# A post-LN transformer block: next batch's q and k made in units 5 and 6, a unit's first step reordered, and the last maxima and sums moved from the FFN's first tile into unit 7

## The reference

```python
def attention(x, w_qkv):                      # x: 8 x 1024 x 512
    q, k, v = split_heads(x @ w_qkv)          # 16 heads of 32
    probs = softmax(q @ k.T / sqrt(512))
    return join_heads(probs @ v)
def fp4_quant_dequant(x):                     # blocks of 16
    scale = maximum(max(abs(block)) / 6, 1e-12)
    return nearest_on_grid(abs(block) / scale) * sign(block) * scale
x = layernorm(x + attention(x, w_qkv))
h = silu(fp4_linear(x, w_gate)) * fp4_linear(x, w_up)     # 512 -> 1408
x = layernorm(x + fp4_linear(h, w_down))                  # 1408 -> 512
```

## Time and profile before

| | us |
|---|---|
| median of 3 runs (lowest, highest) | 4126.7 (4125.9, 4129.7) |
| the profiled execution's own time | 4124.7 |
| its span, first to last instruction | 4123.0 |
| TensorE busy (share of the span) | 3806.5 (92%) |
| VectorE busy | 3051.1 (74%) |
| GpSimd busy | 2283.0 (55%) |
| ScalarE busy | 1749.4 (42%) |
| mean granted clock of TensorE | 0.977 |

### The profile page before, as it was taken

The page is one execution under the profiler, slowest core; times in us unless marked ns, Lnnn a source line. Parts: engine busy times, 40 slices in busy tenths (PEclk is TensorE's granted clock), DMA queues, the critical chain, the costliest instruction groups (busy, mean ns, idle before and its releaser), DMA issues. The chain is left out here.

```text
span 4123.0 us, 61806 instructions
## 1 busy us (share of the span) xinstructions
PE 3806.5 (92%) x22985; PEld 1728.9 (42%) x22985; DVE 3051.1 (74%) x4929; ACT 1749.4 (42%) x3104; POOL 2283.0 (55%) x1446
## 2 busy tenths in 40 slices
PE   3489999999999999999999999999999999999999
PEld 2234344433543345433453434443454334534344
DVE  8866687676876778666786668776786667866787
ACT  3345522664235632455225552265423553245522
POOL 4468722885239832588227862298424883268722
PEclk9689999999999999999999999999999999999999
DMA  4110110111010110111101101101101111010110
GB/s 163 44 58 26 29 50 24 35 32 50 23 35 18 40 44 24 30 32 32 47 19 40 29 21 54 31 22 32 53 22 32 26 34 48 19 37 24 32 49 21
DMA packets 106560, 152.56 MB, mean 37 GB/s; under 512 B 28177, under 2 KB 55569, under 8 KB 106129
## 3 DMA queue, kind: packets, MB, share of 16 engines
q1 hardware_dynamic: 106256, 148.49, 11.6%
HBM read 76.28 MB, written 19.66 MB: 23 GB/s over the span
## 5 line engine op out<-in xcount | busy, mean ns | idle before, releaser
L571 DVE TENSOR_REDUCE mx<-R 128x1 f32<-128x512 f32 x2080 | 1334.4, 686 | 662.6 <-PE R L663 654.6
L1186 ACT ACTIVATE arena<-SC 128x512 f32<-128x512 f32 x1344 | 749.7, 603 | 413.9 <-PE SC L1438 411.0
L1512 PE MATMUL SC<-wgu,split 128*128 128x512 f16 (+1 forms) x3456 | 724.0, 364 | 0.6
L1084 POOL TENSOR_TENSOR wd<-wd,arena 128x1024 f32<-128x1024 f32 x208 | 485.7, 2357 | 31.0 <-ACT arena L1186 29.9
L1110 POOL TENSOR_TENSOR arena<-arena,sc_h 128x704 f32<-128x704 bf16 (+2 forms) x136 | 176.1, 1312 | 576.8 <-DVE arena L496 576.8
L1186 ACT ACTIVATE wd<-SC 128x512 f32<-128x512 f32 x704 | 399.8, 603 | 201.1 <-PE SC L1438 196.9
L1512 PEld LDWEIGHTS SC<-wgu,split 128*128 128x128 f16 x3456 | 338.3, 98 | 343.8 <-issue 12.6
L663 PE MATMUL R<-ks_even,qs_even 96*128 96x512 bf16 x1056 | 398.5, 399 | 88.6 <-issue 45.3
L1227 ACT ACTIVATE arena<-SC,gain 128x512 f32<-128x512 f32 (+1 forms) x192 | 125.1, 652 | 775.0 <-PE R L1512 390.7
L643 PE MATMUL R<-xT,wqkv 128*128 128x512 bf16 x1632 | 429.3, 386 | 11.4 <-DVE split L565 6.5
L663 PE MATMUL R<-arena 96*128 96x512 bf16 x1024 | 368.8, 382 | 17.6 <-DVE xT L558 11.6
(11 more groups left out here) (139 smaller groups left out, 5675.3 us busy)
## 6 DMA issues: line engine op xcount, KB each, us to landing
x<-n_L_attn_embeddings_dram SPq DMA_DIRECT2D x136, 256.0 KB, 2.9
wd<-wd_kept SPq DMA_DIRECT2D x32, 512.0 KB, 5.6
out_dram<-x SPq DMA_DIRECT2D x64, 256.0 KB, 2.0
ks_even<-split SPq DMA_DIRECT2D x204, 64.0 KB, 2.0
qs_even<-split SPq DMA_DIRECT2D x408, 32.0 KB, 1.8
arena<-split SPq DMA_DIRECT2D x192, 64.0 KB, 2.0
arena<-split SPq DMA_DIRECT2D x384, 32.0 KB, 1.8
wd<-wd_kept SPq DMA_DIRECT2D x16, 384.0 KB, 7.5
```

The source lines that it names most:

```text
L571: nc.vector.reduce_max(mx[:, j:j + 1], ring_of(ring, job)[:, :], AX_X).then_inc(max_done, 1)
L1084: nc.gpsimd.tensor_tensor(acc[u % 2][i], first, probs_of(s)[:, hs, :], ALU.add).then_inc(pool_sum, 1)
L1186: nc.scalar.activation(probs_of(s)[:, hd, :], SC[e % SLOTS][:, :], ACT.Exp, scale=SCALE).then_inc(exp_done, 1)
L1512: last = nc.tensor.matmul(GU[kk % 2][which][:, 0:w], xhT[i % 2][:, part_x * KH + k, :], wgu[:, part_w * KH + k, which * I + first:which * ...
```

## The change

It alters the lists and the places, and no operation.

- The first projection of the next batch goes from unit 6 into steps 5 to 7 of unit 5, the second and third stay in unit 6 but at two quarters a step in steps 1 to 4, and the fourth goes from unit 7 into steps 5 and 6 of unit 6.
- In the first step of a unit place 0 comes ahead of the last two `weigh` of the unit before, and ScalarE's `context` behind place 0; the third maximum goes to place 1, the fifth to place 5.
- All 32 maxima of the next batch are in unit 7. `sum`, `neg` and `sumT` stand between unit 7 and the first `gate_up`, `ctx` behind it. These jobs come from the ring of four banks.
- The net's places are renumbered; in tile 0 the turn of x tile 1 stands behind the last `gate_up`.

```diff
@@ -85,12 +85,11 @@
 QUARTERS = 4
 POOL_SUMS = [TILES - 2] * (UNITS - 1) + [TILES // 2]
 MAX_STEPS = (5, 5, 5, 5, 5, 4, 3, 0)
-MAX_STEPS_LAST = (5, 5, 5, 5, 4, 3, 0, 2)
-BEFORE_FFN = sum(MAX_STEPS_LAST)
+MAX_STEPS_LAST = (5, 5, 5, 5, 5, 4, 1, 2)
 MADE = (((1, (4, 5)), (1, 1, 1, 1, 1, 1, 1, 1)), ((2, (0, 1)), (1, 1, 1, 1, 1, 1, 1, 1)),
         ((2, (2, 3, 4)), (2, 2, 2, 1, 1, 1, 2, 1)), ((2, (5,)), (3, (0, 1)), (2, 1, 1, 2, 1, 2, 2, 1)),
-        ((3, (2, 3, 4)), (2, 2, 2, 1, 1, 1, 2, 1)), ((3, (5,)), (4, 0, 0, 0, 0, 0, 0, 0)),
-        ((4, (0, 1, 2)), (0, 3, 3, 2, 2, 2, 0, 0)), ((4, (3, 4)), (2, 2, 1, 1, 1, 1, 0, 0)))
+        ((3, (2, 3, 4)), (2, 2, 2, 1, 1, 1, 2, 1)), ((3, (5,)), (4, (0,)), (4, 0, 0, 0, 0, 1, 1, 2)),
+        ((4, (1, 2, 3)), (0, 2, 2, 2, 2, 2, 2, 0)), ((4, (4,)), (1, 1, 1, 1, 0, 0, 0, 0)))
 SCORES_AT, VALUES_AT = (0, 1, 3, 4), 2
 SUM_STEP, SUM_T_STEP, CTX_STEP = 1, 2, 3
 ADD_TILE, ADD_TILE_LAST = 3, 2
@@ -125,27 +124,26 @@
         other += [("xT", X_TURNS.index((u, t)), 0)]
     neg = [("neg", u + 1, 0)] if t == TILES - 1 and not ends else []
     if t == 0:
-        return m[0:1] + q[0:1] + m[1:2], [], m[2:3], m[3:4] + q[1:2], other + m[4:5], q[2:] + m[5:]
+        return m[0:1] + q[0:1] + m[1:2], m[2:3], [], m[3:4] + q[1:2], other, m[4:5] + q[2:] + m[5:]
     return [], m[0:1] + q[0:1], m[1:2], neg + m[2:3] + other, m[3:4] + q[1:2], m[4:5] + q[2:] + m[5:]
 def first_jobs():
     v = quarters(GROUPS, PROJ_JOBS - 1)
-    return v[0:2] + [("xhT", 0, 0)] + v[2:]
+    return ([("sum", UNITS - 1, 0), ("neg", UNITS, 0)] + v[0:2] + [("xhT", 0, 0)] + v[2:] + [("sumT", UNITS - 1, 0)],
+            [("ctx", UNITS - 1, 0)])
 def tile_jobs(i):
     if i == 0:
-        m = [("max", UNITS, n) for n in range(BEFORE_FFN, MAX_JOBS)]
-        return (m[0:2], m[2:4] + [("sum", UNITS - 1, 0)], m[4:] + [("xhT", 1, 0)],
-                [("sumT", UNITS - 1, 0), ("ctx", UNITS - 1, 0), ("neg", UNITS, 0)], [])
+        return [], [], [("xhT", 1, 0)], []
     turns = [("hT", i - 1, n) for n in range(len(CHUNKS))]
     if i == TILES - 1:
-        return [], turns[0:1], turns[1:2], turns[2:], [("hT", i, 0)]
-    return [], turns[0:1], turns[1:2], [("xhT", i + 1, 0)] + turns[2:], []
+        return turns[0:1], turns[1:2], turns[2:], [("hT", i, 0)]
+    return turns[0:1], turns[1:2], [("xhT", i + 1, 0)] + turns[2:], []
 def tail_jobs():
@@ -155,7 +153,7 @@
 def ffn_jobs():
-    jobs = first_jobs()
+    jobs = []
     for i in range(TILES):
         for part in tile_jobs(i):
             jobs += part
@@ -987,8 +985,8 @@
         steps = [(u, t) for u in range(UNITS) for t in range(TILES)]
-        ring = Ring([job for u, t in steps for place in unit_jobs(u, t) for job in place], ffn_jobs(), RING, RING_FFN,
-                    2, 1, 1)
+        ring = Ring([job for u, t in steps for place in unit_jobs(u, t) for job in place]
+                    + [job for place in first_jobs() for job in place], ffn_jobs(), RING, RING_FFN, 2, 1, 1)
         with nc.Fori(0, B) as b:
@@ -1120,11 +1118,10 @@
                                 add(u - 1)
                     scale_x(0)
                     inverse_deviation("x", 1)
+                    add(UNITS - 1)
                     for i in range(TILES):
                         if i + 1 < TILES:
                             scale_x(i + 1)
-                        if i == 0:
-                            add(UNITS - 1)
                         if 2 <= i < TILES - 1:
                             inverse_deviation("out", i - 2)
                         if i + 2 < TILES:
@@ -1187,8 +1184,6 @@
                                              scale=SCALE).then_inc(exp_done, 1)
                     for s, (u, t) in enumerate(steps):
-                        if t == 0 and u >= 1:
-                            context(u - 1)
                         if (u, t) == (UNITS - 1, LN_SCALE):
                             first_norm(0)
                         for n, place in enumerate(unit_jobs(u, t)):
@@ -1199,6 +1194,8 @@
                                     sums(g)
                                 elif kind == "xT":
                                     x_transposed(g)
+                            if n == 0 and t == 0 and u >= 1:
+                                context(u - 1)
                             if n in SCORES_AT:
                                 exponentials(s, SCORES_AT.index(n))
@@ -1227,15 +1224,15 @@
                         nc.scalar.activation(sg[:, k % 2, 0:CHUNKS[c][1]], GU[k % 2][0][:, 0:CHUNKS[c][1]],
                                              ACT.Silu, scale=un_gain).then_inc(silu_done, 1)
+                    context(UNITS - 1)
+                    sums(UNITS - 1)
                     x_out(0)
-                    context(UNITS - 1)
                     projected(GROUPS, PROJ_JOBS - 1)
                     first_norm(1)
                     for i in range(TILES):
                         silu(i, 0)
                         silu(i, 1)
                         if i == 0:
-                            sums(UNITS - 1)
                             x_out(1)
                         else:
                             h_out(i - 1, 0)
@@ -1362,17 +1359,15 @@
                         dve.wait_ge(y_added, i + 1)
                         moments("out", i, x1[:, i % 4, :], o_done)
+                    maxima_transposed(UNITS)
                     low_x(0)
+                    reciprocals(UNITS - 1)
+                    context_out(UNITS - 1)
                     for i in range(TILES - 1):
-                        if i == 0:
-                            for j in range(BEFORE_FFN, min(BEFORE_FFN + 2, MAX_JOBS)):
-                                maximum(UNITS, j)
                         gated(i, 0)
                         quantise_x(i + 1)
                         gated(i, 1)
                         if i == 0:
-                            for j in range(BEFORE_FFN + 2, MAX_JOBS):
-                                maximum(UNITS, j)
                             low_x(1)
                         else:
                             low_h(i - 1, 0)
@@ -1381,11 +1376,7 @@
                                 second_moments(i - 2)
                             low_h(i - 1, 1)
                         gated(i, 2)
-                        if i == 0:
-                            reciprocals(UNITS - 1)
-                            context_out(UNITS - 1)
-                            maxima_transposed(UNITS)
-                        else:
+                        if i >= 1:
                             low_x(i + 1)
                             low_h(i - 1, 2)
                         if i + 2 < TILES:
@@ -1483,16 +1474,13 @@
                     for s, (u, t) in enumerate(steps):
                         places = unit_jobs(u, t)
-                        if t == 0 and u >= 1:
-                            weigh(s - 2)
-                            weigh(s - 1)
                         for n, place in enumerate(places):
                             run(place)
+                            if n == (0 if t == 0 else VALUES_AT) and s > 0 and t % 2 == 0:
+                                weigh(s - 2)
+                                weigh(s - 1)
                             if n in SCORES_AT:
                                 scores(u, t, SCORES_AT.index(n))
-                            if n == VALUES_AT and t > 0 and t % 2 == 0:
-                                weigh(s - 2)
-                                weigh(s - 1)
                     weigh(len(steps) - 2)
                     weigh(len(steps) - 1)
@@ -1536,23 +1524,24 @@
                         if c == len(CHUNKS) - 1:
                             last.then_inc(y_done, 1)
-                    run(first_jobs())
+                    run(first_jobs()[0])
                     for i in range(TILES):
                         places = tile_jobs(i)
                         gate_up(i, 0, 0)
-                        run(places[0])
+                        if i == 0:
+                            run(first_jobs()[1])
                         gate_up(i, 0, 1)
                         gate_up(i, 1, 0)
                         gate_up(i, 1, 1)
+                        run(places[0])
+                        gate_up(i, 2, 0)
                         run(places[1])
-                        gate_up(i, 2, 0)
+                        gate_up(i, 2, 1)
                         run(places[2])
-                        gate_up(i, 2, 1)
-                        run(places[3])
                         if i >= 1:
                             down(i - 1, 0)
                             down(i - 1, 1)
-                        run(places[4])
+                        run(places[3])
                         if i >= 1:
                             down(i - 1, 2)
                     i = TILES - 1
```

## The result

| | before | after |
|---|---|---|
| median (lowest, highest), us | 4126.3 (4125.8, 4129.7) | 4070.5 (4070.0, 4070.7) |
| ratio, 95% interval | | 0.9863 [0.9846, 0.9880] |
| profiled execution's own time, its span | 4124.7, 4123.0 | 4070.3, 4068.7 |

What follows compares the result with a forecast made beforehand. TensorE, busy 92% of the span, was taken as the bound, so only its waits and slow running could be gained. Six parts summed to -6.25 us a batch, -50 in eight: 4124.7 - 50 + 2 = 4077 us, range 4057 to 4104.

Steps and rivals of the forecast that it cites:

- part 1: At a unit's start, work ahead of the weighs hides the wait for the last exponential: 3.7 us a batch gained.
- Part 2: q stack lands 4.4 us earlier; TensorE's wait at next batch's first maximum falls to 1.3 us: 3.4 us a batch gained.
- part 4: Second projection at unit 6's start waits 1.1 us for the last turned tile: 0.8 us a batch lost.
- part 3: First projection in unit 5, steps 5 to 7: its quarters fill waits for ScalarE, net 0.2 us a batch gained.
- Part 6: FFN's first tile: sums hide waits, a new 1.6 us wait comes at tile 1; net 0.6 us a batch gained.
- Part 5: Unit 7 loses four quarters and gains three maxima; a chain sets its end: 0.85 us a batch lost.
- the price 0.70, and six units: Each wait for the last exponential at a unit's start costs 0.70 us; six units make 4.2 us.
- the cover is thin: Half of part 1 and all of part 3 return as other waits: 2.5 us a batch, 4097 us; chance 0.15.
- The q stack lands in time: No wait for the q stack at the first maximum: 1.3 us a batch more gained, 4067 us; chance 0.12.
- A clock that falls: The 1.3 us wait before the first maximum brings half clock: 13 us lost, 4090 us; chance 0.13.
- No stack sooner: q lands as today, so TensorE waits 5.4 us instead of 3.2 at the first maximum: 4122 us; chance 0.05.
- Slower: Late last x tile delays k's first DMA past 1917.3, and the queue delays the first maximum; 4144 at 1918.5; chance 0.05.

Runs made afterwards that it cites:

- no refill: The changed kernel with the first step of a unit ordered as before: 4082.2 us, ratio 0.9898.
- q, k: The kernel before with only the new table of projections, making the next batch's q and k in units 5 and 6: 4108.4 us, ratio 0.9957.
- e5_q: The changed kernel with no quarter of the second projection in step 1 of unit 6 and four in step 2: 4068.2 us, ratio 0.9859.
- f4_both: e5_q's edit on the changed kernel, plus the turn of x tile 1 back between tile 0's last two gate_up: 4064.2 us, ratio 0.9858.
- f3_nomade: The changed kernel with the next batch's projections back in their old steps: 4116.0 us, ratio 0.9978.
- e1_refill: The kernel before with only a unit's first step reordered, place 0 ahead of the two weighs: 4134.5 us, ratio 1.0023.

## Why the prediction was right, and where not

The time and its sign were right (4070.5 in a range of 4057 to 4104), and the chains of waits were those named; the sizes of four terms were not. Their errors, +2.1 (part 1), -0.7 (2 and 4), -0.6 (3) and -0.7 us (6), cancel to 0.1, and that is luck. Per batch, from the table by stage:

| part | forecast | measured | from |
|---|---|---|---|
| 1, refilled step | -3.7 | -1.6 | after less no refill |
| 2 and 4, q and k in time, second projection | -2.6 | -3.3 | units 6 and 7, see below |
| 3, first projection in unit 5 | -0.2 | -0.8 | unit 5 of q, k: 1.76 - 2.6 |
| 5, unit 7 | +0.85 | +0.5 | unit 7 at full clock, see below |
| 6, FFN's first tile | -0.6 | -1.3 | silu to tile 1: -1.94, plus 0.65 moved out |
| sum | -6.25 | -6.5 | batch: -6.7 |

**Part 1 failed in the step "the price 0.70, and six units".** The waits did go, 29.0 us to 9.2. But of the six starts three pay: those of units 3, 4 and 5, with 0.69, 0.50 and 0.54 (the stretches of units 2 to 4). The stretch of unit 1 gives nothing (31.74, 31.81), though the wait at its end is gone: the 0.57 us came back as a new wait of 0.45 us for GpSimd, at the sum job in step 1 (L673, 3.6 us in eight). GpSimd is busy for 30.06 us of that stretch, but for 30.94 of unit 3's 34.3 as well, which did pay; no run took GpSimd's work away, so that it bounds unit 1 isn't shown. The start of unit 6 gives 0.1, unit 6 itself a loss of 0.2, with the 0.42 us for ScalarE and the 0.33 for the q stack shown above. The rival "the cover is thin" said 1.85 us of part 1 would come back; 2.1 did. It was right on this half and not on the other, part 3.

**Part 2's chain was right, its wait too long.** The stack of q landed 33.2 us behind unit 6's first exponential (1906.8 less 1873.6) where it had been 37.4: 4.2 sooner, 4.4 forecast. The wait was 0.33 to 0.4 and not 1.3, because TensorE came to the first maximum 33.0 us behind that exponential; the prediction's 1928.0 is 32.0 behind it (1896.0). The step that failed is that 1928.0: it left out part 4's wait (1.04 measured, 1.1 forecast), which lies in unit 6 ahead of that maximum. The landing, forecast at 33.1, left the same wait out and came at 33.2 nevertheless, so "both stacks go 4.4 us earlier" was too little by about as much. This second error was luck, for TensorE makes q too, and what holds it up ahead of q's projection holds up both sides: in e5_q and f4_both 0.5 us less of that wait brought the landing and the maximum each 0.5 us sooner and left the wait for the stack at 0.34 to 0.43.

Unit 6 is 2.35 us shorter with q and k alone (0.2 of it clock: the first batch of the kernel before has 40.33, the others 39.0 to 39.2). The half clock is 0.9 in unit 7, the mean of 29.32 less the 28.41 of batches at full clock; 0.8 was taken. -2.35 - 0.9 is the -3.3 of the table, as near as the rounding goes. That the issues count is borne out: 12 take 7.47 us after too, and the maximum still starts 2.0 us behind the last. By the rule of the Trainium skill quoted there (DMA: Bandwidth & Descriptors, "Issuing engines are not separate DMA queues") the wait would be nought and the time 4067. The measured 0.33 us and 4070.5 are close to that, but not for the rule's reason: the issues still stand with 7.47 us between q's projection and the maximum, as the rows had it.

**Part 3** had a cautious end taken: no row of the trace shows the 0.3 lost to three ring buffers.

**Part 5** holds: unit 7 goes from 28.41 us at full clock to 26.95, 1.46 less with 1.95 us of TensorE's work less. The last weigh waits 1.15 us (L1442, 9.2 in eight).

**Part 6** has its waits right, 1.41 for the 1.6 at tile 1's first gate and 1.56 for the 1.8 at the hidden tile. Wrong was "the stretch at half clock behind it stays", which rests on "1.2 GHz after the 2.21 us wait in every batch": the kernel before has it in the second, fourth, sixth and eighth batch only, those that keep full clock behind the 3.2 us wait. Wrong too was what the stretch costs; the prediction read 1.6 us from one gate. Kernel before, third batch:

```profile
1517.06 0.63 PE L1471 MATMUL R<-identf,arena 128*128 128x128 f32 x4 [2.20 <-POOL arena L1110]
1517.52 2.11 PE L1512 MATMUL SC<-wgu,split 128*128 128x384 f16 x12
...
1523.39 0.66 PE L1461 MATMUL R<-identf,split 128*128 128x128 f32 x4 [1.38 <-DVE arena L1336]
```

The fourth batch has the same wait, a gate of 3.75 us, and its turn of x tile 2 at 2009.40, 6.48 us behind the hidden tile; here the gate takes 2.11 and the same turn comes 6.33 us behind. The slow clock fills a wait for VectorE that is there otherwise. That leaves 0.15 us at this turn and nothing in the tile: tile 1 is 27.16 or 27.17 us in all eight batches.

**The rivals.** "The q stack lands in time" came nearest on the wait, 0.33 us for its nought. Its reason holds: k's 12 issues end at 1897.15, 0.9 us before q's first goes out. "A clock that falls" didn't occur: with 0.33 us in front of the maximum the clock is 1.00 in units 6 and 7 of all eight batches. But the 1.3 us it was about were never there, and the one time that so long a wait stood in front of this maximum (1.55 us, the third batch of e5_q) the clock fell and cost 1.5 us. The prediction gave it 0.13 and counted the clock as full behind 1.3 us; that it stayed full may be owed to the shorter wait, which the prediction didn't have: luck, then, and no merit of its reasoning. In tile 1 a wait of 1.56 us left the clock alone in all eight batches. The rule of the Trainium skill weighed there (TensorE: Matmul & The Clock Gate (Part 1)), that idling brings the throttle back, agrees with that batch of e5_q and not with tile 1.

"No stack sooner" is what the refill does without q and k. With the tail, as the rival has it, that is f3_nomade: a wait of 5.4 us and 4116.0 for the rival's 4122. Without the tail (e1_refill) it is 4134.5, with the same wait; there the clock was low in every batch (0.95 in units 6 and 7, where every second one of the kernel before has 1.00). "Slower" needed k's first DMA later than 1917.3; it went out 5.0 us sooner.
